# Criss-cross attention: values stored by channel tile and image column, row strips loaded in 4 KB pieces, three products for four

## What is computed

```python
q = einsum('bchw,oc->bohw', x, Wq) + bq      # 64 channels
k = einsum('bchw,oc->bohw', x, Wk) + bk      # 64 channels
v = einsum('bchw,oc->bohw', x, Wv) + bv      # 512 channels
eH = einsum('bchw,bcpw->bhwp', q, k)         # along the column, own pixel masked out
eH = where(diag, -inf, eH)
eW = einsum('bchw,bchp->bhwp', q, k)         # along the row
att = softmax(concatenate([eH, eW], axis=3), axis=3)
attH, attW = att[..., :H], att[..., H:]
outH = einsum('bcpw,bhwp->bchw', v, attH)
outW = einsum('bchp,bhwp->bchw', v, attW)
return gamma * (outH + outW) + x
```

## Time and profile before

| | us |
|---|---|
| median of 3 runs | 4679.86 (4664.12 to 4681.54) |
| the profiled execution | 4648.17 |
| its span, first to last instruction | 4646.0 |

### The profile page before, as it was taken

The page is one execution under the profiler, slowest core; times in us unless marked ns, Lnnn a source line. Parts: engine busy times, 40 slices in busy tenths (PEclk is TensorE's granted clock), DMA queues, the critical chain, the costliest instruction groups (busy, mean ns, idle before and its releaser), DMA issues.

```text
span 4646.0 us, 122516 instructions
## 1 busy us (share of the span) xinstructions
PE 3813.5 (82%) x39768; PEld 2805.1 (60%) x39768; DVE 3080.0 (66%) x4371; ACT 1860.9 (40%) x3947; POOL 704.0 (15%) x979
## 2 busy tenths in 40 slices
PE   3997789977899768997789867898778977789777
PEld 1557665566655665566755667555775557745577
DVE  6667566675676756767557676576765767667575
ACT  1554135541355313553145522455314543245431
POOL 0113001130011300113011130111301113011120
PEclk9997789977898878988799787897879978799687
DMA  7765987669876798757977489775897759977599
GB/s 251 236 216 189 297 263 232 204 210 287 258 231 187 227 299 244 231 172 255 294 246 235 147 271 293 240 236 163 265 290 241 233 180 262 289 228 231 176 270 277
DMA packets 1130201, 1109.71 MB, mean 239 GB/s; under 512 B 48528, under 2 KB 979856, under 8 KB 1127824
## 3 DMA queue, kind: packets, MB, share of 16 engines
q1 hardware_dynamic: 1044624, 803.63, 61.2%
q10 hardware_dynamic: 85248, 302.03, 17.9%
HBM read 775.16 MB, written 301.99 MB: 232 GB/s over the span
## 4 chain that ended last, share of the span: by engine, by line
PE 32%; DMA 22%; DVE 13%; issue 13%; ACT 10%; SPq 6%; ACTq 2%; POOL 1%; DVEq 1%; POOLq 0%
DMA v_in<-v_pixel_major 17%; PE banks L1019 10%; PE banks L898 5%; DMA x_raw<-x 4%; PE banks L900 4%; PE banks L899 4%; SPq L389 4%; ACT x_hi L476 3%; PE banks L919 3%; PE banks L916 3%; DVE x_lo L696 3%; DVE acc L874 3%; ACT prob_row L512 2%; DVE nmax L754 2%; DVE xmax_blk L651 2%
## 5 line engine op out<-in xcount | busy, mean ns | idle before, releaser
L860 DVE SCALAR_TENSOR_TENSOR acc<-banks,scales,acc 128x384 f32 x1152 | 862.8, 782 | 540.0 <-PE banks L1019 520.8
L898 PE MATMUL banks<-wv_hi,x_hi 128*128 128x512 f16 x2304 | 881.5, 383 | 231.4 <-DVE x_lo L696 231.4
L1019 PE MATMUL banks<-prob_col,v_in 96*128 96x96 f16 x12288 | 704.1, 225 | 234.1 <-DMA v_in<-v_pixel_major 185.6
L899 PE MATMUL banks<-wv_lo,x_hi 128*128 128x512 f16 x2304 | 880.6, 382 | 0.0
L900 PE MATMUL banks<-wv_hi,x_lo 128*128 128x512 f16 x2304 | 879.7, 382 | 0.0
L1019 PE MATMUL banks<-prob_row,v_in 96*128 96x96 f16 x12288 | 699.1, 224 | 156.9 <-DMA v_in<-v_pixel_major 120.6
L1019 PEld LDWEIGHTS banks<-prob_col,v_in 96*128 96x128 f16 x12288 | 652.9, 109 | 286.5 <-issue 207.0
L570 ACT ACTIVATE acc<-acc,gbv_col (+1 forms) x384 | 358.7, 934 | 1143.1 <-DVE acc L860 1102.0
L1019 PEld LDWEIGHTS banks<-prob_row,v_in 96*128 96x128 f16 x12288 | 650.1, 109 | 199.2 <-issue 98.9
L696 DVE SCALAR_TENSOR_TENSOR x_lo<-x_raw,scales,x_hi 128x1024 f16<-128x1024 f32 x288 | 391.7, 1362 | 548.6 <-ACT x_hi L476 548.6
L427 POOL TENSOR_TENSOR q_low<-qk_f,q_both 64x256 f32 x288 | 191.7, 666 | 3016.3 <-ACT k_hi L495 2992.3
(11 more groups left out here) (90 smaller groups left out, 4405.3 us busy)
## 6 DMA issues: line engine op xcount, KB each, us to landing
v_in<-v_pixel_major SPq DMA_DIRECT2D x768, 384.0 KB, 8.4
x_raw<-x SPq DMA_DIRECT2D x288, 512.0 KB, 4.3
x_next<-x SPq DMA_DIRECT2D x288, 512.0 KB, 3.8
v_pixel_major<-v_out SPq DMA_DIRECT2D x576, 256.0 KB, 2.6
out<-acc ACTq DMA_DIRECT2D x384, 384.0 KB, 5.9
acc<-x ACTq DMA_DIRECT2D x16, 4608.0 KB, 19.0
acc<-x ACTq DMA_DIRECT2D x192, 384.0 KB, 8.9
x_first<-x SPq DMA_DIRECT2D x36, 512.0 KB, 7.5
```

The lines of the kernel that those rows point to most:

```text
L860: nc.vector.scalar_tensor_tensor(out=a, in0=out_bank[m % 4], scalar=scales[:, O_FACTOR:O_FACTOR + 1], in1=a, op0=ALU.mult, op1=ALU.add,).t ...
L898: nc.tensor.matmul(dst, s_hi, m_hi, start=(t == 0), stop=False)
L899: nc.tensor.matmul(dst, s_hi, m_lo, start=False, stop=False)
L1019: last = nc.tensor.matmul(dst[:, g, :], v, parts[o][:, h * G + g, c, :], start=(a == 0 and c == 0), stop=(a == 1 and c == 1),)
```

## The change

Three edits. First, the DRAM tensor of the values is laid out by image, channel tile, image column, image row, so that the pixels of one column, for one channel tile, follow each other in 512-byte pieces (hi and lo of 128 channels). A load of eight row strips needs for each partition (an image column) eight neighbouring rows, 4 KB in one piece. A load of column strips still takes eight pieces of 512 bytes per partition. Second, the store of a value tile of 128 pixels is cut where an image row ends (fragments), always into two DMAs, each with pieces of 512 bytes; the semaphore v_stored counts 32 per tile and not 16. Third, the attention makes three products and leaves out the product of the low half of the values with the low half of the probabilities, so that a group has 12 matmuls and not 16; that part of the sum is no longer computed.

```diff
-    vT = nc.dram_tensor("v_pixel_major", [B, HW, CT * 2 * P], F16, kind="Internal").ap()
+    vT = nc.dram_tensor("v_column_major", [B, CT, W, H, 2 * P], F16, kind="Internal").ap()
     vT_load = {
-        ROW: vT.rearrange("b (h w) (t a) -> b t w h a", w=W, t=CT),
-        COL: vT.rearrange("b (h w) (t a) -> b t h w a", w=W, t=CT),
+        ROW: vT,
+        COL: vT.rearrange("b t w h a -> b t h w a"),
     }
+    vT_store = vT.rearrange("b t w h a -> b h w t a")
+
+    def fragments(px):
+
+        return [(row, max(px, row * W), min(px + P, (row + 1) * W)) for row in range(px // W, (px + P - 1) // W + 1)]
...
-            def store_block(b, i, s):
+            def store_block(b, i, s, jj, d):
 
                 for j in range(PT):
                     k = s * PT + j
+                    px = (2 * d + s) * BLK + j * P
 
                     sp.wait_ge(v_ready, (b * NB + 2 * i) * PT + k + 1 + VTILES)
-                    sp.dma_start(
-                        vT[b, bass.ds((2 * i + s) * BLK + j * P, P), :],
-                        v_out[k][:, :, :, :].rearrange("p t a c -> p (t a c)"),
-                    ).then_inc(v_stored[k], 16)
+                    for row, first, end in fragments(px):
+                        sp.dma_start(
+                            vT_store[b, jj * (4 * G) + row, first - row * W:end - row * W, :, :],
+                            v_out[k][first - px:end - px, :, :, :].rearrange("p t a c -> p t (a c)"),
+                        ).then_inc(v_stored[k], 16)
...
-                                for a in range(2):
-                                    v = v_in[u][:, half * G + g, a, :]
-                                    for c in range(2):
-                                        last = nc.tensor.matmul(
-                                            dst[:, g, :], v, parts[o][:, h * G + g, c, :],
-                                            start=(a == 0 and c == 0), stop=(a == 1 and c == 1),
-                                        )
+                                v_hi, v_lo = v_in[u][:, half * G + g, 0, :], v_in[u][:, half * G + g, 1, :]
+                                p_hi, p_lo = parts[o][:, h * G + g, 0, :], parts[o][:, h * G + g, 1, :]
+                                nc.tensor.matmul(dst[:, g, :], v_hi, p_hi, start=True, stop=False)
+                                nc.tensor.matmul(dst[:, g, :], v_hi, p_lo, start=False, stop=False)
+                                last = nc.tensor.matmul(dst[:, g, :], v_lo, p_hi, start=False, stop=True)
                             last.then_inc(o_mm, 1)
```

More of the change, by code:

```diff
@@ L300, in _ @@
             for k in range(2 * PT):
-                sp.sem_inc(v_stored[k], 16)
+                sp.sem_inc(v_stored[k], 32)
             sp.dma_start(wqk_raw[:, :, :], wqkT.rearrange("(t c) o -> c t o", c=P)).then_inc(weights_loaded, 16)
@@ L369, in double_blocks @@
                                 load_block(b, 2 * i + 2 + s, s)
-                            store_block(b, i, s)
+                            store_block(b, i, s, j, d)
                             if more:
@@ L379, in _ @@
                 for k in range(2 * PT):
-                    wait_alone(sp, v_stored[k], (b + 1) * (NB // 2 * 16) + 16)
+                    wait_alone(sp, v_stored[k], (b + 1) * (NB // 2 * 32) + 32)
                 with sp.Fori(0, CT // 2) as tp:
@@ L390, in _ @@
                                         v_in[u][:, :, :, :].rearrange("p s a c -> p s (a c)"),
-                                        vT_load[o][b, tp * 2 + par, :, bass.ds((i * VU + u) * VS, VS), :],
+                                        (vT_load[ROW][b, tp * 2 + par, :, bass.ds((i * VU + u) * VS, VS), :]
+                                         if o == ROW else
+                                         vT_load[COL][b, tp * 2 + par, :, bass.ds((i * VU + u) * VS, VS), :]),
                                     ).then_inc(v_loaded[u], 16)
@@ L483, in high_v @@
                     act.wait_ge(v_mm, (b * NB + 2 * i) * PT + k + 1)
-                    act.wait_ge(v_stored[k], (b * (NB // 2) + i) * 16 + 16)
+                    act.wait_ge(v_stored[k], (b * (NB // 2) + i) * 32 + 32)
                     nc.scalar.activation(
@@ L542, in _ @@
                 for k in range(2 * PT):
-                    act.wait_ge(v_stored[k], (b + 1) * (NB // 2 * 16) + 16)
+                    act.wait_ge(v_stored[k], (b + 1) * (NB // 2 * 32) + 32)
                 for d in range(BODY):
@@ L797, in _ @@
                 for k in range(2 * PT):
-                    dve.wait_ge(v_stored[k], (b + 1) * (NB // 2 * 16) + 16)
+                    dve.wait_ge(v_stored[k], (b + 1) * (NB // 2 * 32) + 32)
                 for w in range(SP):
```

## The result

The changed kernel takes 4602.1 us (4600.7 to 4609.6) where the kernel before, run beside it, takes 4676.5; the ratio is 0.985 (95% interval 0.983 to 0.987). Run again beside other kernels it was 0.987 (0.985 to 0.990). So it is faster, by 1.3 to 1.5%, about 60 to 75 us; 4528 us, 3.2%, was forecast. The two profiled executions differ by less than the medians: spans of 4646.0 and 4599.6 us, 46 us. The execution before happened to lie 28 us under its median, the one after within 3 us of its own, so I compare stages for where time went and medians for how much.

What follows compares the result with a forecast made beforehand. Transfers were taken to bound the last three channel tiles. From the profiled 4648.2 us, -160 (later phases) + 8 (SP's queue) = 4496, plus 31.7 for the median: 4528 us; range 4440 to 4650, the forecast's own 4490 to 4580.

Steps and rivals of the forecast that it cites:

- What bounds the kernel: Last three channel tiles, 175.9 us per image: transfers bound most phases, VectorE close behind in the last column phase.
- The price of a row load: Later row phases: 4 KB pieces at about 370 GB/s for 228, 8 us less per row phase, 24 per image.
- Rival A: Value loads: contention and place, not length, slow them; 271 GB/s, 3.3 us per row phase, 4609 us; chance 0.10.
- the offset: Whole kernel: 31.7 us added because the median of runs lay that far above the profiled execution.
- What was shed: Six later phases: cheaper row loads take about 4 us off each, 175.9 to 152.9, a gain of 23.0 per image.
- The left-out product: Later phases: 12 matmuls for 16 let phases get below 30.7 us; colder clock costs 3 us per image.
- rival B: Row loads not merged; only shorter matmul groups help, mostly the last row phase; 45 us gain, 4643 us; chance 0.05.
- my end of 4.2 us: Later phases: upper end of the clock's cost per image, phases of 20.8 and 21.6 us becoming 23.3.
- First channel tile, unchanged: First channel tile's two phases: VectorE holds them, so the cut matmuls bring 0, at most 1 us per image.
- Stores and SP: Projection: 512-byte stores stay hidden at a DMA share near 0.84; extra SP issues cost 1 us per image, 8 in all.
- Rival C: Projection: scattered short writes choke it; at half the read rate +34 us per image, 4792 us; chance 0.11.
- The column loads: Column phases: 512-byte pieces at new pitches cost the same, 0; 10% either way would be 6 us per image.

Runs made afterwards that it cites:

- experiment three: Changed kernel with each row load moving its 384 KB as 128 partitions of 3 KB, not 96 of 4 KB (wrong values): 4508.6 us, ratio 0.964.
- The mirror: Changed kernel with values by channel tile, image row, image column: column strips in 4 KB pieces, row strips in 512-byte, one store DMA per tile: 4536.3 us, ratio 0.970.

## Why the prediction was half right

*What bounds the kernel: right.* The transfers bound the last three channel tiles. Making the row loads cheaper by shape alone (experiment three) took 94 us off the changed kernel, and taking a quarter of the matmuls away alone took 14 off the kernel before.

*The price of a row load: the step that failed.* I took 12.7 us for a row phase's loads, between the rates of 1 KB and of 36 KB pieces. Both rows came from 128-partition transfers, the value loads have 96 partitions, and I carried the rate over as if only length counted. By itself the 4 KB piece on 96 partitions runs at 270 GB/s against 244 for 512 bytes: 17.5 us for 19.3, 1.8 us for a phase where 8 stood in the sum. In the kernel, 245 for 228 GB/s, 19.3 for 20.7. Three phases and eight images make 34 to 45 us where 192 stood in the sum. What failed was the size of this term, and not the mechanism: with a shape near the assumed rate, 404 GB/s for 370, the six phases lost 23.6 us for the 23.0 forecast, and the kernel took 4508.6 us.

*Rival A* had this rate within reason (271 GB/s) and 4609 us for 4602 measured. That it came so near is partly luck, as the offset below shows. Its cause was half of it: length hardly counts on 96 partitions. I had given it 0.10, on account of the 228 GB/s with no other traffic, which I read as evidence for length and which was just as good evidence for the partitions. The rule of the Trainium skill on short descriptors ("DMA: Bandwidth & Descriptors", "Why small descriptors are slow (HBM only)") that I set beside it comes out near at 96 partitions (11% measured for 14%, 5 to 18% with the other rates of 96), but at 128 partitions the same eightfold length brings 290 to 411 GB/s, 42%, so it isn't what sets these rates. And the 228 to 348 GB/s that I held against it mixed two things: on 128 partitions alone 512 bytes to 1 KB is 290 to 349.

*What was shed did not all stay.* The phases gave 10.8 us per image on the mean, and 2.9 came back in the gap; 1.0 more went to the projection and 0.8 to the first channel tile, which leaves 6.1, or 49 us in eight images, near the 46 between the two spans. The cheaper row loads account for 4.3 to 5.6 us of the 7.9 that the phases and the gap lost together; what the rest is no run shows. This is the DMA view of the gap after, and its counterpart before, 1786.1 to 1800.9 us:

```profile
q1 hardware_dynamic: 2636, 2.62, 43.9%
q10 hardware_dynamic: 823, 2.23, 30.7%
...
q1 hardware_dynamic: 1629, 1.62, 34.2%
q10 hardware_dynamic: 316, 0.85, 15.1%
```

The last row phase is 7 us shorter, and 2.23 MB of its finished rows are written after it, for 0.85 MB before, beside the next image's first x blocks. In the same stretch TensorE waits for its first split x block 13.0 us for 8.8. No step of the forecast had the output's stores in it as what is late next.

*The left-out product: right that it is worth little, wrong in the reason.* I had it hidden by the transfers, with a cost of 3 us for a colder clock. The clock did fall, 0.78 to 0.64 where it was cut alone. But I also had the cut as what lets the phases get below 30.7 us at all, and that was wrong: with the layout alone and all four products, row phases 2 and 4 take 25.5 and 16.2 us. In the third image the granted clock was 0.95 and 1.00 in them, not at the low level. (12 matmuls of 80 ns in 24 groups are 23.0 us, too, and not the 23.3 that my end of 4.2 us used.) What I said of the last row phase under rival B, that TensorE was the last there, was wrong: 24.5 us with three products, 16.2 with the layout.

*First channel tile, unchanged: right.* 60.2 to 61.0 us; the edit took matmuls from a stage that VectorE holds (32.5 us busy of 33.6 in the column phase).

*Stores and SP: right in sum.* The projection went from 250.4 to 251.4 us for the 1 us forecast, at a DMA share of 0.79 (0.84 forecast, though my own sum, 201 of 250 us, is 0.80). By themselves 512-byte stores move 221 GB/s at a share of 0.87, so a short write is a little cheaper than the 228 at a full share that I priced it by. ScalarE's waits for x blocks rose from 16.3 to 21.0 us in the third image:

```profile
ACT x_hi L485 <- DMA x_raw<-x: 21.0, 14, 2.6
```

The mirror, with the same short pieces but one DMA per tile, has 250.1 us and 17.2 us of such waits. So the cost, such as it is, doesn't go with the length of the pieces. The mirror's pieces also lie side by side in device memory from pixel to pixel, so whether the second DMA or the 48 KB pitch costs it is not shown. Rival C didn't happen.

*The column loads* I left at nothing; by themselves they are 5% slower (247 to 235 GB/s), 1 us a phase, about 3 per image against the gain. This is a price of loads alone; no run measures it in the kernel.

*The offset.* I added 31.7 us for the profiled execution lying under the median. It lay 28 under, but the one after lay at its median. So 28 us of the 74 between the medians are not in the traces at all. Run again, the medians were 59 us apart.

## What to carry to other kernels

A rate is a property of the whole shape of a transfer. Before the rate of one row is given to another transfer, hold all of the shape against it: piece length, pitch and number of partitions; here going from 128 partitions to 96 cost more (411 to 270 GB/s) than eight times the length brought back (244 to 270), and moving a third more bytes on all 128 was faster. When transfers bound a stretch, taking work from TensorE may bring little and lower its clock; and when the last phase before a loop's next round gets shorter, look at what it leaves in the queues for that round.

## What the runs showed of the hardware

- Loads of 4 KB per partition, six in flight, nothing else running: 115 GB/s on 16 partitions (the engines not full), 207 on 32, 156 on 48, 209 on 64, 256 on 80, 257 to 287 on 96, 277 on 112, 411 and 412 on 128.
- Pieces of 512 bytes: 244 GB/s on 96 partitions, 290 on 128; 4 KB: 257 to 287 and 411. On 128 partitions a pitch of 48 KB in device memory between partitions cost nothing (411 GB/s with it and 411 with adjacent rows).
- Two DMAs for one were slower: 48 + 48 partitions 210 GB/s and 64 + 32 partitions 240, for 257 to 287 in one DMA of 96.
- Stores alone: 382 GB/s in 2 KB pieces, 221 in 512-byte pieces of two DMAs a tile (the engines at 87%).
- With a quarter of the matmuls gone from a DMA-bound stretch the granted clock fell from 0.78 to 0.64 and the mean matmul of a row phase went from 232 ns to 260:

```profile
L1019 PE MATMUL banks<-prob_row,v_in 96*128 96x96 f16 x288 | 61.5, 260 | 0.0
```
